# Centring, activation rounding and their small factors move from ScalarE to VectorE, with a new order on all engines

## The reference, cut to what matters

```python
def reference(x, ctx, ...):
    x = x + tanh(g_xattn) * scan_block(ctx, layernorm(x))
    x = x + tanh(g_ffn) * ffn(layernorm(x))

def scan_block(ctx, z):            # B=4, L=256, 256 channels, 16 states
    x = silu(conv(ctx @ in_proj.T) + conv_b)
    dt_low, B, C = split(x_proj @ x)
    dt = softplus(dt_proj @ dt_low + dt_b)
    state = state * exp(dt * A) + (dt * x) * B       # scan over 256 tokens
    y = sum_states(state * C) + D * x
    return y * silu(z)

def quant(x):                      # row by row
    s = 127 / max(|x|)
    return round(x * s) / s

def ffn(x):                        # hidden 704
    x1, x3 = split(quant(x) @ w13.T)
    gated = relu(x1)**2 * x3
    inner = gated * rsqrt(mean(gated**2) + 1e-5) * norm_w
    return quant(inner) @ w2.T
```

## Time and profile before

| what | value |
|---|---|
| runs | 161.07, 161.22, 163.43 us |
| profiled execution, own time | 163.65 us |
| its span, first to last instruction | 161.8 us |
| busy | PE 93%, ACT 88%, DVE 76%, POOL 76% |
| mean granted TensorE clock | 0.979 of full |

### The profile page before, as it was taken

One profiled execution on the slowest core, in us unless ns is written; L12 is line 12 of the kernel. 1 busy time (PEld: TensorE's weight loads), 2 busy tenths in 40 slices (PEclk: granted clock), 3 DMA queues, 4 the chain that ended last, 5 costly groups with the idle time before them and its releaser, 6 DMA issues.

```text
span 161.8 us, 3705 instructions
## 1 busy us (share of the span) xinstructions
PE 150.4 (93%) x1298; PEld 119.3 (74%) x1298; DVE 122.9 (76%) x158; ACT 142.3 (88%) x361; POOL 122.4 (76%) x117
## 2 busy tenths in 40 slices
...
GB/s 112 375 358 243 113 254 329 17 78 242 222 39 40 2 54 223 232 221 61 4 2 169 249 215 203 208 4 0 2 36 0 2 36 0 32 0 4 34 65 65
DMA packets 26500, 18.39 MB, mean 114 GB/s; under 512 B 13481, under 2 KB 21106, under 8 KB 26354
## 3 DMA queue, kind: packets, MB, share of 16 engines
...
q10 hardware_dynamic: 288, 0.16, 0.3%
...
## 4 chain that ended last, share of the span: by engine, by line
ACT 43%; PE 29%; DMA 11%; issue 9%; DVE 4%; SPq 2%; POOL 1%; ACTq 0%; DVEq 0%; POOLq 0%
ACT dA L629 26%; PE w_ps L1013 8%; DMA b_diag<-low 5%; PE w_ps L997 5%; DMA bd<-b_diag 5%; PE m_ps L941 3%; PE w_ps L905 3%; PE w_ps L888 2%; ACT ru L691 2%; ACT duT L647 2%; DVE xc L752 2%; PE y_ps L872 2%; PE w_ps L897 2%; SPq L501 2%; DVE hb L799 1%
## 5 line engine op out<-in xcount | busy, mean ns | idle before, releaser
L799 DVE TENSOR_TENSOR_SCAN hb<-dA,m_ps 128x1024 f32<-128x1024 f32 x32 | 71.9, 2274 | 7.8 <-PE m_ps L941 4.7
L431 POOL TENSOR_TENSOR hb<-hb,cs 128x1024 f32<-128x1024 f32 x31 | 73.0, 2367 | 6.3 <-DVE hb L799 5.8
L629 ACT ACTIVATE dA<-dt,nega 128x255 f32<-128x255 f32 (+1 forms) x160 | 59.4, 454 | 0.0
L941 PE MATMUL m_ps<-bd,duT 64*128 64x128 f32 (+1 forms) x448 | 38.0, 311 | 2.9 <-DMA bd<-b_diag 1.3
L941 PEld LDWEIGHTS m_ps<-bd,duT 64*128 64x128 f32 x448 | 30.5, 197 | 9.8 <-issue 5.9
L967 PE MATMUL y_ps<-identf,hb 128*128 128x128 f32 x256 | 32.4, 275 | 0.2 <-DVE hb L431 0.2
L967 PEld LDWEIGHTS y_ps<-identf,hb 128*128 128x128 f32 x256 | 27.9, 140 | 2.6 <-issue 1.0
L997 PE MATMUL w_ps<-wT,xqT 128*128 128x352 bf16 x64 | 20.3, 318 | 0.5 <-ACT xqT L684 0.5
L997 PE MATMUL w_ps<-wres,xqT 128*128 128x352 bf16 x64 | 20.3, 317 | 0.0
L997 PE MATMUL w_ps<-wlo,xqT 128*128 128x352 bf16 x64 | 19.8, 310 | 0.0
L445 POOL TENSOR_TENSOR gw<-gg,normw 128x704 f32<-128x704 f32 x7 | 11.8, 1691 | 3.2 <-DVE gg L837 3.2
...
## 6 DMA issues: line engine op xcount, KB each, us to landing
...
```

Source lines behind the costliest of these rows:

```text
L431: E.tensor_tensor(h_g, h_g, cs[:, :, s0:s0 + sn, l0:l0 + ln], ALU.mult).then_inc(hc_end if (b, i, h) == OUT_END else hc_ok[h], 1)
L629: last = act_fn(dA_g[:, r, s, 1:ln], dt[:, b, h, l0 + 1:l0 + ln], ACT.Exp, scale=nega[:, h, at:at + 1])
L799: V.tensor_tensor_scan(hb[:, k % 3, h], decays, m_ps[:, h], 0.0, ALU.mult, ALU.add).then_inc(scan_ok[h], 1)
L941: last[r] = T.matmul(m_r[:, :, c * Q - l0:(c + 1) * Q - l0], duT[rows, p, h, (c - r) % CHUNKS, :], bd[rows, c, gs[0]:gs[-1] + 1].rearrange ...
```

## The change

xn, quant1 and quant2 leave ScalarE's list and code and come into VectorE's, with the same inputs, outputs and waits. The arithmetic of each is one two-operation tensor_scalar: (x - mean) * -1, xn * fs + 1536, gw * gc + 1536; fs and gc are tensor_scalar on one or two columns, finv is one tensor_tensor in place of one activation a tile. All five lists have a new order; the steps in them are otherwise the same ones. The code:

```diff
@@ -655,26 +654,6 @@
                     link(act_fn(frs[:, b, ts], fmv[:, b, ts, 1], ACT.Ln, bias=const[:, 0:1]))
                     act_fn(xn[:, ts, L], frs[:, b, ts], ACT.Exp, scale=0.5, bias=const[:, 1:2])
                     act_fn(frs[:, b, ts], frs[:, b, ts], ACT.Exp, scale=-0.5, bias=const[:, 3:4]).then_inc(frs_ok, 1)
-                elif name == "xn":
-
-                    act.wait_ge(fmv_ok, b + i + 1)
-                    if b == 0:
-                        act.wait_ge(work_full, full("inproj", BATCH - 1, 0))
-                    for t in tiles(b, i):
-                        last = act_fn(xn[:, t, 0:L], x[:, b, t], ACT.Identity, scale=-1.0, bias=fmv[:, b, t, 0:1])
-                    last.then_inc(xn_ok, 1)
-                elif name == "quant1":
-                    act.wait_ge(fs_ok, b + i + 1)
-                    if b:
-                        act.wait_ge(work_full, full("xqT", b - 1, 0))
-                    ts = slice(tiles(b, i)[0], tiles(b, i)[-1] + 1)
-                    link(act_fn(fs[:, b, ts], fr[:, b, ts], ACT.Copy, scale=127.0))
-                    for t in tiles(b, i):
-                        act_fn(xq[:, t], xn[:, t, 0:L], ACT.Identity, scale=fs[:, b, t:t + 1],
-                               bias=const[:, 2:3]).then_inc(xq_ok, 1)
-                    for t in tiles(b, i):
-                        last = act_fn(finv[:, b, t:t + 1], fam[:, b, t:t + 1], ACT.Copy, scale=frs[:, b, t:t + 1])
-                    last.then_inc(finv_ok, 1)
                 elif name == "xqT":
                     act.wait_ge(work_full, full("xqT", b, i))
                     if b:
@@ -705,15 +684,6 @@
                     link(act_fn(grs[:, b, hs], ssq[:, b, hs], ACT.Ln, scale=1.0 / HID, bias=const[:, 0:1]))
                     act_fn(gw[:, hs, HID], grs[:, b, hs], ACT.Exp, scale=0.5, bias=const[:, 1:2])
                     act_fn(grs[:, b, hs], grs[:, b, hs], ACT.Exp, scale=-0.5).then_inc(grs_ok, 1)
-                elif name == "quant2":
-                    act.wait_ge(gc_ok[i], b + 1)
-                    if b == 0:
-                        act.wait_ge(iq_zero, 1)
-                    else:
-                        act.wait_ge(work_full, full("iqT", b - 1, i))
-                    link(act_fn(gc[:, b, i:i + 1], gr[:, b, i:i + 1], ACT.Copy, scale=127.0))
-                    act_fn(iq[:, i, 0:HID], gw[:, i, 0:HID], ACT.Identity, scale=gc[:, b, i:i + 1],
-                           bias=const[:, 2:3]).then_inc(iq_ok[i], 1)
                 elif name == "iqT":
                     act.wait_ge(work_full, full("iqT", b, i))
                     if b:
@@ -819,6 +789,14 @@
                     for h in range(t0, t1):
                         last = V.bn_aggr(fmv[:, b, h], fstat[:, h])
                     last.then_inc(fmv_ok, 1)
+                elif name == "xn":
+
+                    dve.wait_ge(fmv_ok, b + i + 1)
+                    if b == 0:
+                        dve.wait_ge(work_full, full("inproj", BATCH - 1, 0))
+                    for t in tiles(b, i):
+                        last = V.tensor_scalar(xn[:, t, 0:L], x[:, b, t], fmv[:, b, t, 0:1], -1.0, ALU.subtract, ALU.mult)
+                    last.then_inc(xn_ok, 1)
                 elif name == "fam":
                     t0, t1 = tiles(b, i)[0], tiles(b, i)[-1] + 1
                     ts = slice(t0, t1)
@@ -826,6 +804,24 @@
                     dve.wait_ge(frs_ok, b + i + 1)
                     link(V.tensor_reduce(fam[:, b, ts], xn[:, ts, :], AX.X, ALU.max, apply_absolute_value=True))
                     V.reciprocal(fr[:, b, ts], fam[:, b, ts]).then_inc(fs_ok, 1)
+                elif name == "quant1":
+                    dve.wait_ge(fs_ok, b + i + 1)
+                    if b:
+                        dve.wait_ge(work_full, full("xqT", b - 1, 0))
+                    ts = slice(tiles(b, i)[0], tiles(b, i)[-1] + 1)
+                    link(V.tensor_scalar(fs[:, b, ts], fr[:, b, ts], 127.0, None, ALU.mult))
+                    for t in tiles(b, i):
+                        V.tensor_scalar(xq[:, t], xn[:, t, 0:L], fs[:, b, t:t + 1], ROUND, ALU.mult, ALU.add).then_inc(xq_ok, 1)
+                    V.tensor_tensor(finv[:, b, ts], fam[:, b, ts], frs[:, b, ts], ALU.mult).then_inc(finv_ok, 1)
+                elif name == "quant2":
+                    dve.wait_ge(gc_ok[i], b + 1)
+                    if b == 0:
+                        dve.wait_ge(iq_zero, 1)
+                    else:
+                        dve.wait_ge(work_full, full("iqT", b - 1, i))
+                    link(V.tensor_scalar(gc[:, b, i:i + 1], gr[:, b, i:i + 1], 127.0, None, ALU.mult))
+                    V.tensor_scalar(iq[:, i, 0:HID], gw[:, i, 0:HID], gc[:, b, i:i + 1], ROUND,
+                                    ALU.mult, ALU.add).then_inc(iq_ok[i], 1)
                 elif name == "gate":
                     h, c = i // 2, i % 2
                     dve.wait_ge(work_full, full("up", b, i, 1))
```

VectorE's list, whole (the lists are compared from the first scan on; - before, + after):

```diff
-        conv/0.0 conv/0.1 lowc/0.0 xstat/0.0 lowc/1.0 du/0.0 du/0.1 bT/0.0 bd/0.0 scan0/0.0 scan1/0.0 scan0/0.1
-        conv/2.0 scan1/0.1 conv/3.0 scan0/0.2 lowc/2.0 lowc/3.0 scan1/0.2 scan0/0.3 scan1/0.3 scan0/1.0 scan1/1.0
-        yz/0.0 x1/0.0 scan1/1.1 scan0/1.1 fam/0.0 scan1/1.2 scan0/1.2 scan1/1.3 scan0/1.3 scan1/2.0 scan0/2.0 gate/0.0
-        gate/0.1 scan0/2.1 yz/1.0 x1/1.0 scan1/2.1 fam/1.0 gate/0.2 scan0/2.2 scan1/2.2 gate/0.3 scan0/2.3 scan1/2.3
-        absmax/0.0 gate/1.0 scan0/3.0 gate/1.1 scan1/3.0 yz/2.0 x1/2.0 absmax/0.1 gate/1.2 scan1/3.1 scan0/3.1
-        gate/1.3 fam/2.0 scan1/3.2 final/0.0 scan0/3.2 yz/3.0 x1/3.0 absmax/1.0 gate/2.0 absmax/1.1 gate/2.1 scan0/3.3
-        gate/2.2 final/0.1 fam/3.0 scan1/3.3 out1/3.3 gate/2.3 yz/3.1 x1/3.1 final/1.0 fam/3.1 absmax/2.0 gate/3.0
-        gate/3.1 absmax/2.1 gate/3.2 gate/3.3 final/1.1 absmax/3.0 gated/3.1 absmax/3.1 final/2.0 final/2.1 final/3.0
-        final/3.1
+        conv/0.0 conv/0.1 lowc/0.0 xstat/0.0 bT/0.0 du/0.0 bd/0.0 lowc/1.0 du/0.1 scan0/0.0 scan1/0.0 scan0/0.1
+        scan1/0.1 conv/2.0 scan1/0.2 conv/3.0 scan0/0.2 lowc/2.0 lowc/3.0 scan1/0.3 scan0/0.3 scan0/1.0 scan1/1.0
+        yz/0.0 x1/0.0 scan0/1.1 xn/0.0 scan1/1.1 scan0/1.2 fam/0.0 scan1/1.2 quant1/0.0 scan0/1.3 scan1/1.3 gate/0.0
+        scan0/2.0 scan1/2.0 scan0/2.1 yz/1.0 scan1/2.1 x1/1.0 scan0/2.2 gate/0.1 scan1/2.2 xn/1.0 fam/1.0 gate/0.2
+        quant1/1.0 gate/0.3 scan0/2.3 scan1/2.3 absmax/0.0 absmax/0.1 gate/1.0 scan0/3.0 quant2/0.0 gate/1.1 scan0/3.1
+        scan1/3.0 gate/1.2 yz/2.0 quant2/0.1 x1/2.0 scan1/3.1 final/0.0 gate/1.3 xn/2.0 scan0/3.2 fam/2.0 final/0.1
+        quant1/2.0 scan1/3.2 scan0/3.3 gate/2.0 yz/3.0 scan1/3.3 x1/3.0 gate/2.1 gate/2.2 absmax/1.0 xn/3.0 out1/3.3
+        fam/3.0 quant1/3.0 quant2/1.0 gate/2.3 absmax/1.1 quant2/1.1 yz/3.1 gate/3.0 x1/3.1 xn/3.1 gate/3.1 fam/3.1
+        quant1/3.1 final/1.0 absmax/2.0 quant2/2.0 final/1.1 absmax/2.1 quant2/2.1 gate/3.2 absmax/3.0 gate/3.3
+        gated/3.1 quant2/3.0 absmax/3.1 final/2.0 quant2/3.1 final/2.1 final/3.0 final/3.1
```

ScalarE's list around the end of batch 0, then TensorE's around the same place and at its end, GpSimd's from out1/1.0 on, SyncE's start:

```diff
-        duT/0.0 decay0/0.0 duT/0.1 decay1/0.0 decay0/0.1 xrs/0.0 decay1/0.1 tap/2.0 ud/0.0 decay0/0.2 tap/3.0
-        decay0/0.3 decay1/0.2 tab/0.3 u/2.0 z/0.0 u/3.0 z/1.0 z/2.0 z/3.0 tab/0.4 soft/1.0 soft/2.0 soft/3.0 tab/0.5
-        decay1/0.3 duT/1.0 decay0/1.0 duT/1.1 decay1/1.0 szT/0.0 decay0/1.1 ud/1.0 decay1/1.1 decay0/1.2 xn/0.0
+        xrs/0.0 duT/0.0 decay0/0.0 duT/0.1 decay1/0.0 decay0/0.1 ud/0.0 tap/2.0 decay1/0.1 decay1/0.2 decay0/0.2
+        decay0/0.3 tap/3.0 decay1/0.3 tab/0.3 u/2.0 z/0.0 z/1.0 u/3.0 z/2.0 z/3.0 tab/0.4 soft/1.0 soft/2.0 soft/3.0
+        tab/0.5 duT/1.0 duT/1.1 decay0/1.0 decay1/1.0 szT/0.0 ud/1.0 decay1/1.1 duT/2.0 decay0/1.1 decay1/1.2 szT/1.0
...
-        mix0/0.2 warm/0.5 skip/0.0 sum0/0.0 sum0/0.1 sum1/0.0 mix1/0.2 xdbl/2.0 xdbl/3.0 dtproj/1.0 dtproj/2.0
-        dtproj/3.0 mix0/0.3 szT/0.0 mix1/0.3 duT/1.0 sum1/0.1 duT/1.1 sum0/0.2 mix0/1.0 mix1/1.0 sum1/0.2 sum0/0.3
+        warm/0.5 skip/0.0 sum0/0.0 mix1/0.2 mix0/0.2 sum1/0.0 sum0/0.1 sum1/0.1 mix1/0.3 xdbl/2.0 xdbl/3.0 dtproj/1.0
+        dtproj/2.0 dtproj/3.0 mix0/0.3 szT/0.0 duT/1.0 duT/1.1 sum0/0.2 mix0/1.0 mix1/1.0 sum1/0.2 sum1/0.3 duT/2.0
...
-        xqT/2.0 sum1/3.1 sum0/3.1 mix0/3.3 up/2.0 up/2.1 skip/3.1 up/2.2 down/0.1 iqT/1.0 sum1/3.2 sum0/3.2 up/2.3
-        sum0/3.3 xqT/3.0 iqT/1.1 sum1/3.3 down/1.0 up/3.0 up/3.1 xqT/3.1 up/3.2 up/3.3 iqT/2.0 down/1.1 iqT/2.1
-        down/2.0 down/2.1 iqT/3.0 iqT/3.1 down/3.0 down/3.1
+        sum1/3.1 xqT/2.0 mix0/3.3 up/2.0 sum0/3.1 mix1/3.3 up/2.1 up/2.2 skip/3.1 sum1/3.2 up/2.3 sum0/3.2 sum0/3.3
+        xqT/3.0 sum1/3.3 iqT/1.0 up/3.0 iqT/1.1 up/3.1 down/1.0 xqT/3.1 down/1.1 up/3.2 up/3.3 iqT/2.0 iqT/2.1
+        down/2.0 iqT/3.0 down/2.1 iqT/3.1 down/3.0 down/3.1
...
+        du/2.0 out0/0.3 out0/1.0 du/3.0 out1/1.0 out0/1.1 out1/1.1 out0/1.2 out0/1.3 out1/1.2 out1/1.3 out0/2.0
```

(7 more changed lines are left out.)

44 lines of the change are left out of this document (19 added, 25 removed).

## The result

The kernel after takes 168.54 us (median of 4 runs, 167.23 to 169.09), before 162.17 us beside it (4 runs, 161.07 to 163.43): ratio 1.038, 95% interval 1.027 to 1.049. The forecast was 161.0 with a range of 156 to 166, so the time lies 2.5 us above the range. Ratios here are of undisturbed runs alone, so they need not be the quotient of the medians. The profiled execution of after has an own time of 169.09, a span of 167.1 (before 161.8) and a mean granted clock of 0.959.

A forecast was written before the change was run, and what follows sets the result against it. All five engines looked nearly full, TensorE fed nearly all the time; a 2.5 us early lead made 4.3 us at the last scan, given back in the tail, so the end moved from 159.65 to about 159.4: 161.0 us, range 156.0 to 166.0.

The forecast's parts named there:

- wrong altogether: Signs that would refute the whole prediction: a last scan after 134, or a tail longer than 30 us behind it.
- What bounds the kernel: Whole kernel: TensorE is fed nearly all the time; relieving ScalarE gives back little more than TensorE's waits, largest 0.5 us.
- Up to the second batch: Start up to scan0/1.0: order alone brings it from 50.36 to 47.9, a lead of 2.5 us, bounds 0 and 3.5.
- Durations: Moved steps on VectorE: 0.42 us for 256 columns, 0.89 for 704, 0.17 for small factors, 16.9 us in all.
- lower end: Low side of the moved steps' durations: 0.164 us fixed part; with the rest halved, 0.29 for 256 columns, 0.53 for 704.
- short-and-free: Faster rival, 156.8 us: moved operations on VectorE take 0.29 and 0.53 us and meet nobody; chance 0.32.
- From scan0/1.0 to the last scan: Middle stage on VectorE: busy 79.3 plus 2.8 us idle, so the last scan ends at 130.0, before 134.3.
- The tail: Behind the last scan: 6.1 us until xqT/3.0, then 23.4 us of TensorE's steps; end at 159.5, before 159.65.
- two chains that tie: Behind the last scan: VectorE's chain, 29 to 30 us, was put level with TensorE's.
- The slower rival: VectorE's moved steps and GpSimd's outs hold each other up, two to four whole outs, 5 to 10 us; 165.0, chance 0.25.
- The lead is lost: Before batch 1's scans: low clock lasts longer or bget/1.0 lands late, 2.5 us missing; 163.0, chance 0.07.
- The sum: Whole kernel: last instruction moves from 159.65 to about 159.4, giving 161.0 us; median of before's runs was 161.22.

The follow-up runs named there:

- early_after: Before, with all five lists up to batch 1's first scan taken from after and nothing moved off ScalarE; 164.64 us, ratio 1.021.
- ports: Separate kernel timing single VectorE operations with GpSimd idle, then busy: tensor_scalar from SBUF to SBUF 0.28 then 1.85 us, at 704 columns 0.52 then 2.60.
- early_before_xn_unheld: After, with before's lists up to batch 1's first scan and the centring alone in the tensor_scalar form that also sums its output; 163.79 us, ratio 1.014.

## Why the prediction was wrong, step by step

- **Where the miss sits.** The time is 7.5 us above the forecast: 4.9 in the start of batch 1's scans (52.75 for 47.9), -0.1 in the middle stage, 0.6 in the tail, which makes 164.86 for the last final instead of 159.4, and some 2 in the step from there to a time. Both signs of "wrong altogether" came, a last scan after 134 (134.74) and a tail over 30 us (30.1).
- **What bounds the kernel** held. TensorE's own work is the same, and the 5.3 us are what it lost more. That ScalarE's relief gives back little held too, more strongly than put: no run gained from it.
- **Up to the second batch** failed. I forecast a lead of 2.5 us, with bounds of 0 and 3.5 (scan0/1.0 at 47.9); it came 2.4 us late, at 52.75. I laid the steps out at full-clock durations and expected one low stretch, where before had it. The new order has two: one of 3.4 us at 17.2 behind gaps of 0.38 and 0.45 us, and one of 6.8 us at 44.5. The bound of 0 had no reason in the rows: nothing there excluded a loss. early_after shows this part alone at some 3.4 us. And 50.36 was itself late for before's lists, which mostly give 48.9, so the order costs more than the 2.4 us.
- **Durations.** Free, the steps take 0.33 to 0.43 (centring), 0.35 and 0.59 (roundings) and 0.15 us, close to the lower end. From 256 to 704 columns a tensor_scalar grows by 0.24 us in ports and in after, and the rows with two inputs that I bounded it by grow by 0.48. The Trainium skill, "VectorE: DVE Perf Modes", section on the perf-mode tier table, states just this half for a tensor_scalar on fp32 in SBUF; the runs agree, in the part that grows with the width. I took the row of the same width, and called width the rule though all rows behind it were of other operations. (The 5.2 us that the prediction gives for it come to 5.0: 16 x 0.13 + 8 x 0.36.) In ports and here, the one-input form from SBUF to SBUF is both: short, and held by GpSimd. I gave short-and-free a chance of 0.32 as a rival of its own, but the two came together.
- **From scan0/1.0 to the last scan**, 82.1 forecast and 82.0 measured, is right by chance: the roundings and small factors are 1.4 us shorter than forecast, the centrings 3.1 longer, the idle time 2.6 against 2.8, and the other 1.6 us that VectorE was spared come from its other steps.
- **The tail**, 29.5 forecast and 30.1 measured, held, with xqT/3.0 and the last sum behind each other as described. But TensorE is busy nearly throughout and waits 0.2 us for xqT/3.0's input, where I expected it to idle; it is its own order that makes the tail long, not two chains that tie.
- **The slower rival** (VectorE and GpSimd hold each other, 165.0) was the right mechanism. It named xn/0.0, xn/1.0, quant2/0.0, quant2/0.1 and xn/2.0; xn/0.0 and xn/1.0 were held, 3.1 us in all, not 8. It was to decide from 4.2 us of waits on; here 3.1 us more than forecast cost 3.1 in time. It was priced on VectorE alone, without what TensorE's idling can do to its clock. *The lead is lost* was the other half of the truth, at 163.0 with no loss beyond the lead. Both came, and the forecast weighed them as alternatives.
- **The sum.** With both causes taken away (early_before_xn_unheld) the last final ends at 159.71, beside a forecast of 159.4; the time is then 163.79 and not 161.0. That the two ends agree is partly luck: the forecast starts from a trace of before with 6.8 us at the lower clock, this kernel's has 3.4. The rest is that I took 161.0 from that trace, whose execution had 163.65 with a clock of 0.979, and set the median of 161.22 beside it: 2.4 us of a low-clock execution were left out of the sum. At the same clock, 0.989, single runs of before beside this kernel's take 161.1 to 162.1 and this kernel 163.7 to 163.8. So some 2 us remain to the new order: 3.5 more lost up to xqT/1.0 (a rounding held for 1.2 of it), 1.8 less behind. Which steps make the rest of it stays open.
